# A bound on the row index of the key/value gather in a graph-attention kernel

## The reference

```
q, k, v = x @ Wq.T + bq, x @ Wk.T + bk, x @ Wv.T + bv     # per node, 64 values each
logits  = (q[dst] * k[src]).sum(-1) / sqrt(16)            # per edge and head
m       = segment_max(logits, dst)
e       = exp(logits - m[dst])
alpha   = e / segment_sum(e, dst)[dst]
out     = segment_sum(v[src] * alpha, dst) + x @ Ws.T + bs
```

## Time and profile before

| | |
|---|---|
| median of 3 runs | 3585.76 us (3584.13 to 3588.15) |
| the profiled execution's own time | 3588.15 us |
| its span in the profile | 3586.4 us |
| busy: PE / DVE / ACT / POOL | 2470.6 / 2396.9 / 1117.9 / 1938.3 us |
| gathers at L542 | 1664, 1673.5 us busy |
| first and last gather of layer 1 | start at 197.43 us and 1284.27 us |
| first and last gather of layer 2 | start at 1460.59 us and 2551.80 us |
| granted TensorE clock, whole span | 0.741 |

### The profile page before, as it was taken

One profiled execution on the slowest core, in us unless ns is written; L12 is line 12 of the kernel. 1 busy time (PEld: TensorE's weight loads), 2 busy tenths in 40 slices (PEclk: granted clock), 3 DMA queues, 4 the chain that ended last, 5 costly groups with the idle time before them and its releaser, 6 DMA issues. The chain is left out here.

```text
span 3586.4 us, 47557 instructions
## 1 busy us (share of the span) xinstructions
PE 2470.6 (69%) x13243; PEld 2120.5 (59%) x13243; DVE 2396.9 (67%) x3615; ACT 1117.9 (31%) x2130; POOL 1938.3 (54%) x1958
## 2 busy tenths in 40 slices
PE   1536666666566655266656566666589999999999
PEld 1425555555455544255545454555479989989998
DVE  3347777777777864387777777877655656556565
ACT  6301111111111111011111111111156656666666
POOL 6567777777777747677777777777410000000000
PEclk9756666666666655566666656666589999999999
DMA  9334444444454423344445454544300000000000
GB/s 377 129 96 134 123 132 131 126 131 124 127 129 128 129 66 81 88 137 138 128 128 138 129 137 131 142 133 135 91 17 11 13 25 11 13 24 1 21 11 11
DMA packets 394170, 356.45 MB, mean 99 GB/s; under 512 B 88694, under 2 KB 327436, under 8 KB 394080
## 3 DMA queue, kind: packets, MB, share of 16 engines
q1 hardware_dynamic: 221360, 168.40, 15.6%
q0 software_dynamic: 62896, 125.63, 14.4%
q10 hardware_dynamic: 109824, 61.36, 5.6%
HBM read 246.90 MB, written 108.30 MB: 99 GB/s over the span
## 5 line engine op out<-in xcount | busy, mean ns | idle before, releaser
L542 POOL DMA_INDIRECT kv<-kv_table,ix x1664 | 1673.5, 1006 | 530.9 <-issue 493.4
L553 PE MATMUL kT<-identity,kv 128*128 128x128 f32 x832 | 360.1, 434 | 916.8 <-DMA kv<-kv_table,ix 916.8
L649 ACT ACTIVATE ex<-gap 128x1024 f32<-128x1024 f32 x208 | 219.8, 1057 | 1742.1 <-DVE gap L625 1741.8
L553 PEld LDWEIGHTS kT<-identity,kv 128*128 128x128 f32 x832 | 182.6, 219 | 940.0 <-DMA kv<-kv_table,ix 686.6
L603 DVE TENSOR_TENSOR_SCAN held_q<-mask,held_q,qT 128x512 f32<-128x512 bf16 x208 | 265.9, 1278 | 485.9 <-PE qT L554 484.8
L1323 DVE TENSOR_TENSOR hid_lo_x<-full_x,hid_hi_x 128x448 fp32r<-128x448 f32 x448 | 276.0, 622 | 261.3 <-ACT hid_hi_x L1209 254.7
L1209 ACT ACTIVATE full_x<-psH_x,offset_x,scale_x 128x448 f32<-128x448 f32 x448 | 331.6, 740 | 285.2 <-PE psH_x L1064 285.1
L560 PE MATMUL logit<-kq,head_sum 128*128 128x512 f32 x416 | 389.9, 1040 | 2.6 <-DVE gap L625 2.6
L1013 POOL DMA_DIRECT2D x_x<-in_x x7 | 6.8, 971 | 631.4 <-DVE total_x L1367 631.4
L554 PE MATMUL qT<-identity,qz 128*128 128x128 f32 x832 | 346.5, 417 | 0.0
L577 PE MATMUL restT<-pick,top 128*128 128x8 f32 x1664 | 337.5, 275 | 0.0
(11 more groups left out here) (209 smaller groups left out, 5240.1 us busy)
## 6 DMA issues: line engine op xcount, KB each, us to landing
running_sums<-rows ACTq DMA_DIRECT2D x208, 288.0 KB, 4.5
qz<-q_at_starts SPq DMA_DIRECT2D x208, 256.0 KB, 3.2
mask<-masks SPq DMA_DIRECT2D x416, 128.0 KB, 3.8
q_at_starts<-zeros SPq DMA_DIRECT2D x16, 1664.0 KB, 18.7
kv<-kv_table,ix POOLq DMA_INDIRECT x1664
x_sb<-in_x SPq DMA_DIRECT2D x1, 6272.0 KB, 27.6
kv_table<-proj SPq DMA_DIRECT2D x14, 448.0 KB, 3.2
x_x<-in_x POOLq DMA_DIRECT2D x7, 896.0 KB, 5.8
```

The lines of the kernel that those rows point to most:

```text
L542: pool.indirect_dma_start(kv[:, u, j, 2 * HC * s:2 * HC * (s + 1)], None, kv_t, bass.IndirectOffsetOnAxis(ix[:, u, n:n + 1], 0)).then_inc( ...
L553: pe.transpose(kT[u % 2][:, P * j:P * (j + 1)], kv[:, u, j, 0::2], identity[:, :])
```

## The change

The gather at L542 gets a bound on its index, as the other indirect DMAs of the kernel have one.

```
@@ -540,7 +540,8 @@
                                 for s in range(STREAMS):
                                     n = STREAMS * j + s
                                     pool.indirect_dma_start(kv[:, u, j, 2 * HC * s:2 * HC * (s + 1)], None, kv_t,
-                                                            bass.IndirectOffsetOnAxis(ix[:, u, n:n + 1], 0)).then_inc(kv_in[u], 16)
+                                                            bass.IndirectOffsetOnAxis(ix[:, u, n:n + 1], 0),
+                                                            bounds_check=NP - 1, oob_is_err=False).then_inc(kv_in[u], 16)
                     each_step(pool, body)
```

## The result

The changed kernel takes 3702.06 us (median of 4 runs, 3693.03 to 3706.64), beside 3586.95 us for the kernel before in the same comparison. The ratio on record is 1.0306, with a 95% interval of 1.028 to 1.0333: slower by 3.1%. The two medians are 115 us apart. The prediction said 3672 us, 3630 to 3710, slower. The sign, the place and most of the amount came as forecast; some 30 us more were lost than the central value said, and the time lies 8 us inside the upper end of the range.

The account below looks back on a forecast made before the run. POOL's back-to-back issue of L542's gathers was taken to bound the edge phases, 61% of the span. 1664 gathers at 51 ns add 84.9 us, moves and stretches 0: 3672 us from 3588.15 profiled and 3585.76 median, range 3630 to 3710.

Parts of the forecast that it names:

- POOL's issue of gathers is the pace of the edge phases: Both edge phases: POOL issues L542's gathers back to back, never waits for a buffer, and sets 61% of 3588 us.
- The price, 51 ns from L276: Each of L542's 1664 gathers: a bound adds 51 ns, read from bounded gather L276, 84.9 us in all.
- the scatter (25 ns) and the gather of 16 rows (below nothing): Lower bounds on the bound's price at L542: bounded scatter L126, +42 us; bounded gather of 16 rows, -13 us.
- The register move is hidden: POOL's sequencer before each gather: the 29 ns move runs under the present gather and costs nothing.
- The stretched gathers, 0 with 25 us to either side: Gathers at L542 held by DVE instructions, 90 us before: total forecast unchanged, likeliest within 25 us.
- the prediction's own sign: Check at L542: median 1000 to 1005 ns but time off by over 25 us means the stretched-gathers step failed.
- the band of 3648 to 3698 that had the 78%: Whole kernel: 51 ns on each gather with stretches within 25 us, 3648 to 3698 us, chance 78%.
- What lies outside: Setup, node phase and expert phase: no instruction of L542 there, so no change forecast.
- Half the price (26 ns): Rival at L542: the bound costs half, as the bounded scatter suggests, 3630 us; 9% together with halved stretches.
- no price: Rival at L542: the check runs beside other work, median stays 952 ns, 3588 us; chance 5%.
- The move on the path: Rival on POOL's sequencer: register moves add 48.3 us, 3721 us; 6% together with dearer by the phase.
- The phase against DVE: Rival at L542: more gathers caught, +48 us, 3721 us, 6% with the move; or fewer, -45 us, 3628 us.

Follow-up runs that it names:

- the pair without collisions: Kernel before and changed kernel, each with four DVE instructions reading one input from PSUM instead of SBUF: 3508.11 us without the bound, 3596.23 us with it.
- moves_only: Kernel before, gather still without a bound, plus the changed kernel's register move ahead of each gather: 3976.23 us, ratio 1.0003.
- psum_before: Kernel before, no bound, its four DVE instructions with two SBUF inputs reading one from PSUM instead: 3508.11 us, ratio 0.9704.

## Why the prediction was right

- *POOL's issue of gathers is the pace of the edge phases.* Right on the chip of the result: the phases grew by exactly what L542's busy time grew, 112.9 us, and POOL's waits stayed at 530 us. The step held because its test, that POOL never waits for a buffer, was read from the rows. It does not hold on every chip, which no row of the profile of before tells.
- *The price, 51 ns from L276.* 55 ns were measured (1007 - 952), and 53 ns, 88 us, in the pair without collisions. The neighbour with the same shape, number of rows and row length was the right price tag, 4 ns off; the scatter (25 ns) and the gather of 16 rows (below nothing) were not. The size of this term was off by 6.6 us.
- *The register move is hidden.* Right: 0.305 us between gathers in both, moves_only keeps the gather at 955 ns, and the pair without collisions leaves no time for the moves.
- *The stretched gathers, 0 with 25 us to either side.* They grew by 21.4 us, near the end of that band. This is the term of the sum that was mis-sized most. By the prediction's own sign the step failed: the median came out 2 ns above the 1000 to 1005 that it named, and the time is off by 30 us, more than 25. The two stretches grew by 53 and 59 us where 42 each were forecast, and PE's wait by 121 us where it was 85. The 3702 us lie 4 us outside the band of 3648 to 3698 that had the 78%. The price's 6.6 us and the stretches' 21.4 us missed in the same direction; the wide range held both. The mechanism was named rightly, and psum_before shows it; the reasoning for the 0 was weak at one point. I argued that the number of DVE instructions that can hold a gather is fixed, so the total stays. That number held, but the total is set by how many gathers they catch and for how long: 329 for 89 us before, 248 for 111 us after. A gather that slips in ahead of three instructions of a block can meet the fourth just after its start, for 0.94 us. Three unbounded gathers end at most 0.04 us behind that start, three bounded ones up to 0.13 us. The period of bounded gathers, 1.30 us, and the starts of the DVE instructions were in the trace of before. That these two explain the 50 long gathers follows from the counts in the two traces; no run tried a period in between where POOL is the pace.
- *What lies outside.* Node phase +1.3, expert phase +6.7 us in the profiled execution, where nothing was forecast; the timed medians differ by 115.1 us, 2.2 more than the edge phases alone, so most of those 8 us seem to be that execution's own.
- *The rivals.* Half the price (26 ns) and no price fell by the median of 1007. The move on the path fell by the gap. The phase against DVE was a part of the result, with about half of the 48 us it was given.

## What to carry to other kernels

If an engine issues one kind of instruction back to back for most of the span, price a change to that instruction by its nearest relative in the same trace (same shape, with the option), and check that the engine's waits are near zero; then the product is the answer. If another engine can hold it, lay the starts of both side by side with the new period: a few per cent on one side can bring an instruction just behind the start of a long hold that it used to slip past. And a price on one engine is paid only where that engine is the pace, which can differ from chip to chip for the same program.

## What the runs showed of the hardware

- A DVE instruction with two inputs in SBUF holds a gather that POOL starts during it, until its end; with one of the inputs in PSUM, of the same length, it holds none (greatest gather 1462 ns before, 1022 in psum_before; 193 of 193 gathers that start well inside were held before, none of 326 in psum_before). In the traces of before and after a gather that starts up to 0.04 to 0.06 us after the start of such an instruction is not held. This agrees with the rule of the Trainium skill, "SBUF — State Buffer", section "Who interferes with whom", that the prediction drew on; the rule speaks of two inputs in SBUF against a GpSimd instruction that reads SBUF, and the gather reads its indices there.
- A bound on the index costs an indirect gather of 128 rows 53 to 55 ns on POOL (952 to 1005 and 1007). On another chip it is 955 ns without and 1007 with it, 1021 with out-of-bounds as an error, and 1017 where every second gather is unbounded. All indices here were in bounds.
- The same program took 3587, 3617, 3973 and 3974 us in four comparisons. On the last two, ACT waited 364 to 546 us, in the eight kernels profiled there, for events that the profile calls remote, ahead of a copy whose waits are PE and an earlier store, and a change worth 3.1% elsewhere was worth 1.0004 (0.9988 to 1.0019).
